# Marks of two edge sorts split over VectorE, ScalarE and GpSimd, and chunks placed one batch later on TensorE

## The reference

```python
logits = jax.nn.leaky_relu(al_s[src] + al_d[dst], 0.2)
alpha = _segment_softmax(logits, dst, num_nodes)
msg = h[src] * alpha[:, :, None]
out = jax.ops.segment_sum(msg, dst, num_segments=num_nodes)
```

## Time and profile before

| | us |
|---|---|
| median of 3 runs | 13213.7 (13208.91 to 13229.04) |
| profiled execution, its time | 13124.58 |
| its span | 13122.8 |
| busy in the span: DVE | 8087.8 |
| busy in the span: PE | 7310.8 |
| busy in the span: POOL | 5296.6 |
| busy in the span: ACT | 580.3 |
| counting loops | 174.5 and 175.1 |
| ranking loops | 1028.0 and 1028.1 |

### The profile page before, as it was taken

How to read it: one execution, slowest core, us unless ns; L and a number is a source line. 1 busy time by engine, 2 the same in 40 slices (tenths; PEclk the granted TensorE clock), 3 DMA queues, 4 the chain that set the end, 5 groups by cost and what they waited for, 6 DMA issues and landing times. The chain is left out here.

```text
span 13122.8 us, 152037 instructions
## 1 busy us (share of the span) xinstructions
PE 7310.8 (56%) x32826; PEld 4771.1 (36%) x32826; DVE 8087.8 (62%) x27204; ACT 580.3 (4%) x2200; POOL 5296.6 (40%) x5059
## 2 busy tenths in 40 slices
PE   4555355568886455556665466666666433333335
PEld 2333233344444344433333234444443323223333
DVE  9999899957777444445665666666664322332224
ACT  0000000010001000001000100000001000000001
POOL 0000000046662566615777033333330666556670
PEclk6777677765655555557666776666665555555557
DMA  0111111133332221213444133333330111211111
GB/s 18 50 50 51 38 50 50 53 93 107 106 106 53 60 43 42 42 10 105 114 111 110 64 113 112 112 112 111 111 102 31 45 45 45 38 20 23 23 23 22
DMA packets 456540, 857.24 MB, mean 65 GB/s; under 512 B 136865, under 2 KB 197974, under 8 KB 455766
## 3 DMA queue, kind: packets, MB, share of 16 engines
q0 software_dynamic: 226304, 550.69, 17.4%
q1 hardware_dynamic: 229718, 300.70, 7.8%
HBM read 798.81 MB, written 52.14 MB: 65 GB/s over the span
## 5 line engine op out<-in xcount | busy, mean ns | idle before, releaser
L954 POOL DMA_INDIRECT all_Y<-table,te_index x832 | 851.1, 1023 | 1384.9 <-DVE all_Y L1123 1177.1
L954 POOL DMA_INDIRECT all_Y<-table,a1e_index x832 | 891.3, 1071 | 454.6 <-issue 245.4
L954 POOL DMA_INDIRECT all_Y<-table,be_index x832 | 942.0, 1132 | 292.9 <-issue 245.8
L954 POOL DMA_INDIRECT all_Y<-table,a2e_index x832 | 833.0, 1001 | 515.5 <-DVE all_Y L1123 293.1
L1330 POOL DMA_INDIRECT g2e_rows<-table,g2e_index x832 | 839.6, 1009 | 447.1 <-issue 247.8
L1330 POOL DMA_INDIRECT g1e_rows<-table,g1e_index x832 | 815.4, 980 | 481.5 <-issue 236.0
L994 PE MATMUL te_ps_u<-all_Y,te_onehot 128*128 128x264 f32 x1664 | 749.1, 566 | 458.1 <-DVE all_Y L1123 384.2
L1123 DVE TENSOR_TENSOR all_Y<-all_Y 128x512 f32<-128x512 f32 (+1 forms) x1664 | 964.6, 580 | 40.3 <-issue 18.1
L994 PE MATMUL be_ps_u<-all_Y,be_onehot 128*128 128x258 f32 x1664 | 722.7, 572 | 430.0 <-DVE all_acc L1135 257.5
L994 PE MATMUL a1e_ps_u<-all_Y,a1e_onehot 128*128 128x264 f32 x1664 | 878.8, 654 | 83.8 <-DVE all_acc L1135 47.2
L1346 PE MATMUL g1e_ps_u<-g1e_rows,g1e_onehot 128*128 128x128 f32 x1664 | 485.1, 444 | 757.8 <-issue 478.3
(11 more groups left out here) (464 smaller groups left out, 15600.2 us busy)
## 6 DMA issues: line engine op xcount, KB each, us to landing
all_Y<-lows SPq DMA_DIRECT2D x196, 256.0 KB
all_Y<-codes SPq DMA_DIRECT2D x196, 256.0 KB
a1e_place_row<-places_dst SPq DMA_DIRECT2D x104, 256.0 KB
a2e_place_row<-places_dst SPq DMA_DIRECT2D x104, 256.0 KB
be_place_row<-places_src SPq DMA_DIRECT2D x104, 256.0 KB
te_place_row<-places_src SPq DMA_DIRECT2D x104, 256.0 KB
all_Y<-table,a1e_index POOLq DMA_INDIRECT x832
all_Y<-table,a2e_index POOLq DMA_INDIRECT x832
```

The costliest lines, as they stand in the source:

```text
L954: pool.indirect_dma_start(out=rows[:, r, k, :], out_offset=None, in_=table, in_offset=bass.IndirectOffsetOnAxis(ap=index[:, r, k:k + 1], a ...
```

## The change

In the counting loop DVE makes five of the eight low marks and ACT three: ACT takes the absolute difference of lane number and low part (`Abs`), three instructions of 128 columns, and then one `Relu` of 1 minus that, 384 columns. PE waits for both engines.

In the ranking loop ACT makes all low marks in that way, eight `Abs` and one `Relu` of 1024 columns, two batches ahead, and after them copies the eight values of that batch per partition from `other_t` into `carried`. POOL makes the row marks, eight `tensor_scalar` instructions a batch, from `row` (DVE) and `carried` (ACT). DVE keeps the column marks, now one behind the other, and has six of the next batch's `earlier` instructions in pairs where the low marks were, two at the end. In PE's step t the chunks of batch t-1 are placed, four ahead of the starts of t+1 and four behind; the last batch is placed after the loop. There are new semaphores for it, and two new buffers (`away`, `carried`).

```diff
--- before.py
+++ after.py
@@ -252,6 +252,7 @@
         m = Memory(nc, stack, f"count_{name}")
         in_acc = Region(acc)
         low1 = [in_acc.take(8, P, dt=F16) for _ in range(2)]
+        away = in_acc.take(8, P, dt=F16)
         window1 = [in_acc.take(8, WIN, dt=F16) for _ in range(2)]
         count = in_acc.take(WIN)
         groups = in_acc.take(WIN)
@@ -271,7 +272,8 @@
         ps_b = [m.ps(f"ps_b{h}", [P, 512]) for h in range(2)]
         s_marks, s_counted, s_count, s_sums, s_step, s_ends, s_turned, s_end, s_end1, s_windows = (m.sem(x) for x in (
             "marks", "counted", "count", "sums", "step", "ends", "turned", "end", "end1", "windows"))
-        s_hot, s_started, s_starts, s_prefix = (m.sem(x) for x in ("hot", "started", "starts", "prefix"))
+        s_hot, s_started, s_starts, s_prefix, s_away, s_late = (m.sem(x) for x in ("hot", "started", "starts", "prefix", "away", "late"))
+        SPLIT = 5
         with nc.Block() as block:
             @block.vector
             def _(dve):
@@ -279,7 +281,7 @@
                     wait(dve, s_counted, t - 1)
                     dve.tensor_tensor(window1[b], bc(lane16[:, 0:WIN].rearrange("p (k w) -> p k w", k=1), [P, 8, WIN]),
                                       bc(window_t[:, bass.ds(t * 8, 8)].rearrange("p (k w) -> p k w", w=1), [P, 8, WIN]), ALU.is_equal)
-                    for k in range(8):
+                    for k in range(SPLIT):
                         last = dve.tensor_scalar(low1[b][:, k, :], lane16[:, 0:P], low_t[:, bass.ds(t * 8 + k, 1)], None, ALU.is_equal)
                     last.then_inc(s_marks, 1)
 
@@ -332,10 +334,27 @@
                 link(dve.tensor_tensor_scan(starts, total, bc(c.zero[:, :], [P, NSLOT]), -1.0, ALU.add, ALU.add))
                 link(dve.tensor_tensor(place, place, starts, ALU.add))
 
+            @block.scalar
+            def _(act):
+                def marks(t, b):
+                    wait(act, s_late, t)
+                    for k in range(SPLIT, 8):
+                        act.activation(away[:, k, :], lane16[:, 0:P], ACT.Abs, scale=-1.0, bias=low_t[:, bass.ds(t * 8 + k, 1)]).then_inc(s_away, 1)
+                    wait(act, s_counted, t - 1)
+                    act.wait_ge(s_away, t * (8 - SPLIT) + (8 - SPLIT))
+                    act.activation(low1[b][:, SPLIT:8, :], away[:, SPLIT:8, :], ACT.Relu, scale=-1.0, bias=1.0).then_inc(s_late, 1)
+
+                marks(0, 0)
+                marks(1, 1)
+                with act.Fori(1, NB // 2) as i:
+                    marks(i * 2, 0)
+                    marks(i * 2 + 1, 1)
+
             @block.tensor
             def _(pe):
                 def tally(t, b, first=False, final=False):
                     pe.wait_ge(s_marks, t + 1)
+                    pe.wait_ge(s_late, t + 1)
                     for k in range(8):
                         last = pe.matmul(ps_c[:, 0:WIN], low1[b][:, k, :], window1[b][:, k, :], start=first and k == 0, stop=final and k == 7)
                     last.then_inc(s_counted, 1)
@@ -376,6 +395,7 @@
         code_row = [in_y.take(8 * P, dt=F16) for _ in range(2)]
         turned = [in_y.take(8 * P, dt=F16) for _ in range(2)]
         low1 = [in_y.take(8, P, dt=F16) for _ in range(2)]
+        away = in_y.take(8, P, dt=F16)
         window1 = [in_acc.take(8, WIN, dt=F16) for _ in range(2)]
         ahead = [in_acc.take(8, WIN, dt=F16) for _ in range(2)]
         picked = in_acc.take(8, WIN)
@@ -395,7 +415,8 @@
         s_turned, s_earlier, s_marks, s_prefix, s_ahead, s_total, s_high, s_base, s_start, s_picked, s_started, s_slot, s_scaled, s_column, s_row, s_hot, s_placed = (
             m.sem(x) for x in ("turned", "earlier", "marks", "prefix", "ahead", "total", "high", "base", "start", "picked", "started", "slot",
                                "scaled", "column", "row", "hot", "placed"))
-        s_step, s_passed = m.sem("step"), m.sem("passed")
+        carried = [in_acc.take(8) for _ in range(2)]
+        s_step, s_passed, s_away, s_low, s_value, s_valued, s_passed_pool = (m.sem(x) for x in ("step", "passed", "away", "low", "value", "valued", "passed_pool"))
 
         def batches(eng, step):
             step(0, 0)
@@ -432,8 +453,8 @@
                 def arrived(t, b):
                     dve.wait_ge(s_rows[b], t * 16 + (32 - 16 * b))
 
-                def earlier_in_chunk(t, b):
-                    for k in range(8):
+                def earlier_in_chunk(t, b, k0, k1):
+                    for k in range(k0, k1):
                         dve.scalar_tensor_tensor(same[:, k, :], code_row[b][:, k * P:(k + 1) * P], code_t[:, bass.ds(t * 8 + k, 1)], before,
                                                  ALU.is_equal, ALU.mult, accum_out=earlier[b][:, k:k + 1]).then_inc(s_earlier, 1)
 
@@ -458,45 +479,32 @@
                         dve.tensor_tensor(low16, base, high16, ALU.subtract).then_inc(s_base, 1)
                     if then:
                         dve.tensor_tensor(window1[n], bc(lane16[:, 0:WIN].rearrange("p (k w) -> p k w", k=1), [P, 8, WIN]),
-                                          bc(window_t[:, bass.ds(u * 8, 8)].rearrange("p (k w) -> p k w", w=1), [P, 8, WIN]), ALU.is_equal)
-
-                    def low_marks(k0, k1):
-                        for k in range(k0, k1):
-                            last = dve.tensor_scalar(low1[n][:, k, :], lane16[:, 0:P], low_t[:, bass.ds(u * 8 + k, 1)], None, ALU.is_equal)
-                        if k1 == 8:
-                            last.then_inc(s_marks, 1)
-
+                                          bc(window_t[:, bass.ds(u * 8, 8)].rearrange("p (k w) -> p k w", w=1), [P, 8, WIN]), ALU.is_equal).then_inc(s_marks, 1)
                     if now:
                         dve.wait_ge(s_started, t + 1)
                         dve.wait_ge(s_earlier, (t + 1) * 8)
                         dve.tensor_tensor(slot, start, earlier[b], ALU.add).then_inc(s_slot, 1)
                     if then:
-                        low_marks(0, 2)
+                        earlier_in_chunk(u, n, 0, 2)
                     if now:
                         dve.wait_ge(s_slot, t + 1)
                         dve.tensor_scalar(scaled, slot, 1.0 / P, -0.5 + 0.5 / P, ALU.mult, ALU.add).then_inc(s_scaled, 1)
                     if then:
-                        low_marks(2, 4)
+                        earlier_in_chunk(u, n, 2, 4)
                     if now:
                         dve.wait_ge(s_scaled, t + 1)
                         dve.tensor_scalar(column[b], scaled, MAGIC, -MAGIC, ALU.add, ALU.add).then_inc(s_column, 1)
                     if then:
-                        low_marks(4, 6)
+                        earlier_in_chunk(u, n, 4, 6)
                     if now:
                         dve.wait_ge(s_column, t + 1)
+                        wait(dve, s_valued, t * 8 - 8)
                         dve.scalar_tensor_tensor(row[b], column[b], -float(P), slot, ALU.mult, ALU.add).then_inc(s_row, 1)
-                    if then:
-                        low_marks(6, 8)
-                    if now:
                         for k in range(8):
                             wait(dve, s_placed, t * 8 + (k - 15))
-                            dve.tensor_scalar(column1[b][:, k, :], lane16, column[b][:, k:k + 1], None, ALU.is_equal)
-                            if k == 0:
-                                dve.wait_ge(s_row, t + 1)
-                            dve.tensor_scalar(row1[b][:, k, :], lane16[:, 0:P], row[b][:, k:k + 1], other_t[:, bass.ds(t * 8 + k, 1)],
-                                              ALU.is_equal, ALU.mult).then_inc(s_hot, 1)
+                            dve.tensor_scalar(column1[b][:, k, :], lane16, column[b][:, k:k + 1], None, ALU.is_equal).then_inc(s_hot, 1)
                     if then:
-                        earlier_in_chunk(u, n)
+                        earlier_in_chunk(u, n, 6, 8)
 
                 step(-1, 1)
                 batches(dve, step)
@@ -516,17 +524,44 @@
 
             @block.scalar
             def _(act):
+                def low_marks(u, b):
+                    wait(act, s_low, u)
+                    for k in range(8):
+                        act.activation(away[:, k, :], lane16[:, 0:P], ACT.Abs, scale=-1.0, bias=low_t[:, bass.ds(u * 8 + k, 1)]).then_inc(s_away, 1)
+                    act.wait_ge(s_away, u * 8 + 8)
+                    act.activation(low1[b], away, ACT.Relu, scale=-1.0, bias=1.0).then_inc(s_low, 1)
+                    wait(act, s_valued, u * 8 - 8)
+                    act.activation(carried[b], other_t[:, bass.ds(u * 8, 8)], ACT.Copy).then_inc(s_value, 1)
+
                 def step(t, b):
                     act.wait_ge(s_prefix, t + 1)
                     wait(act, s_start, t - 1)
                     act.activation(ahead[b].rearrange("p k w -> p (k w)")[:, WIN:8 * WIN], ps_r[b][:, WIN:8 * WIN], ACT.Copy).then_inc(s_ahead, 1)
-
+                    if exists(t + 2):
+                        low_marks(t + 2, b)
+
```

(28 more changed lines are left out.)

## The result

The changed kernel takes 13909.3 us (median of four runs, 13893.7 to 13911.8) against 13211.3 for the kernel before, also of four. The ratio is 1.0536, with a 95% interval of 1.0499 to 1.0573: 5.4% slower, where the forecast was 1.1% faster. (A ratio given here is the middle of its interval; the quotient of the medians can differ by 0.001 to 0.002, here it is 1.0528.) The profiled execution has a span of 13908.1 us.

A forecast was written before the change was run, and what follows sets the result against it. VectorE (DVE) was taken to bound both sorts' loops, with POOL the new ranking bound. Ranking -90, counting -69 and ends +12 gave -147 us from 13213.7, rounded 13,070 us; the 8-in-10 range was 12,780 to 13,390.

The forecast's parts named there:

- The ring: Ranking loop: DVE to `row`, POOL's eight marks, ACT's two copies, PE's starts, DVE wait in turn; 6.03 + 8p us a batch.
- 8p: Ranking loop: time of POOL's eight row marks in a batch, taken as 4.0 us.
- p: Ranking loop: distance between starts of two POOL row marks, taken as 0.50 us; at 0.56 the batch equals today's 10.49.
- high end: Ranking loop: a POOL mark that also waits for one DVE column mark each time, 0.47 + 0.35 = 0.82 us.
- POOL's begin: Ranking loop: delay from the end of DVE's `row` to POOL's first mark, 0.33 us.
- The starts: Ranking loop: PE's starts of the next batch, 0.74 us plus about 0.1 for first load and hand-over, 0.85 us.
- Rival 4: Ranking loop: PE's starts run at 1.2 GHz, 0.36 us more a batch, gain eaten; 13,140 to 13,240 us, chance 0.10.
- rival 2: Ranking loop: POOL's marks and DVE's column marks take turns at the port, 0.64 to 0.82 us each; 13,380 us, chance 0.33.
- Rival 3: Ranking loop: POOL is cheap, p = 0.29, ring 8.35 us; 12,740 us, or 12,560 at DVE's floor; chance 0.22.
- Counting: Counting loop: ACT's three `Abs` and one `Relu` set the batch at 1.43 us instead of 1.78, 69 us less in all.
- The ends: Ends of each sort: last batch placed after its last marks, first low marks ahead of first prefix; 12 us more in all.
- DVE's floor: Ranking loop: DVE keeps 7.4 us of work a batch; if it stayed the bound, 598 us would go.

The follow-up runs named there:

- e2: Changed kernel with the copy into `carried` made by DVE just ahead of `row` instead of by ACT; 12743.9 us, ratio 0.9659 to the kernel before.
- e4: Kernel before plus a block ahead of the sorts with POOL marks of several kinds; the mark takes 0.78 us alone, 1.1 beside DVE's column marks.
- e10: Changed kernel with twelve more 512-column matmuls a batch on PE ahead of the starts; 13762.5 us against 13135.9 for the kernel before, ratio 1.0485.
- e1: Changed kernel with row marks back on DVE and no `carried` copy; 12909.8 us against 13188.1 for the kernel before, ratio 0.9786.
- e7: e2 with six low marks of the counting loop on DVE and two on ACT; 12059.9 us, ratio 0.9609 to the kernel before.

## Why the prediction was wrong

**The mechanism was right.** The ring named in the prediction (DVE to `row`, POOL's marks, ACT's two copies, PE's starts) is the one that sets the batch; e2 cuts it, and 5.8 us a batch go. The time of a batch is a sum of the form that I wrote, a fixed part and 8p, but both parts were too small, so that the true break-even lies below the p = 0.56 that I gave.

**The failed step is the term 8p, the price of a POOL mark.** It stood at 4.0 us (p = 0.50, high end 0.82) and measured 7.31. Of the 3.3 us too little, 2.2 are POOL's own price (0.775 instead of 0.50) and 1.1 come from DVE's work beside it, nearly all from the column marks. I took the price per column of a `tensor_scalar` from a cast and added two reads for the pointers. e4 shows which half failed: the two pointers cost 0.14 us, near the 0.18 that I had put in, but "the comparison costs nothing extra" was wrong. With constants in place of pointers the mark still takes 4.9 / 8 = 0.61 us where the cast takes 0.29, and it grows by 3.3 ns a column instead of 0.8. Even my high end was too low, because it rested on the same row; and by the formula p = 0.82 makes 12.59 us a batch and 13,570 us, which the range, cut at 13,390, did not hold either. So the range failed although p was named as the open quantity: no row of the trace had this operation on POOL, and here the cast was only a lower bound.

**The other terms of the ring.** DVE's 4.19 us measured 4.17. ACT's copies, 0.66, measured 0.69. POOL's begin, 0.33, took 0.48; three waits stand ahead of the first mark, but no run takes them apart. The starts, 0.85, took 1.45, at the lower clock. Rival 4 had named this and priced it at 0.36 more, which is what came back from 1.45 to 1.09 in the turns of e10 whose clock rose. The other 0.24 is a reading that was too low at either clock. Together these add 0.15 + 0.60 + 0.03 - 0.02 = 0.76 us to the 3.3, and 10.03 becomes 14.10. They are small beside 8p, but they alone would have turned the sign. With 6.79 in place of 6.03 the break-even is p = 0.46, so that my p of 0.50 would have given 10.79 us a batch: 196 x 0.30 = 59 us more, less 21 for the counting, about 13,250 us. That lies in the range and is slower than the kernel before, not faster.

**The rivals.** The sign was that of rival 2, but not its cause or size. It would have had 13,380 us, with turns of 0.70 each. Of its signs one came, marks over 0.6 us apart, and the other did not: the column marks lasted 0.44 us as before. The port costs 0.14 us a mark here; if it had cost nothing, the ring would still have been 13.0 us a batch and the kernel slower. The Trainium skill (SBUF — State Buffer, "Who interferes with whom") has the second to issue blocked for the whole instruction of the other. The runs agree that the two interfere, and in both directions, but three column marks passed in one POOL mark of e4 (24 in 8.8 us, eight POOL marks beside them). So they do not take turns instruction by instruction, and with column marks POOL waits more than DVE. Rival 3 (cheap POOL) was the opposite of what came. Rival 4's sign came (the starts took over 1 us), as a part of the loss.

**Counting.** 21 us came instead of 69. A batch is 1.67 us, not 1.43: the `Abs` lasts 0.39 and the next starts 0.29 later. My row for it was a copy from PSUM with no pointer. The estimate from the Trainium skill (ScalarE: Activation LUTs, "What ACT_TABLE_LOAD costs"), 1.67 us, was the measured value. For the three `Abs` that is the page's price (0.39 us at 128 columns, each next one 0.29 later); that the whole fits to 0.01 us is partly luck, as the `Relu` took 0.52 us and the hand-over 0.17, which I had not measured. The row had been the wrong one.

**The ends.** They were priced at 12 us and cost about 2: PE's last placing starts at 3284.9 instead of 2597.0 us, 688 us later, of which 686 are the loops.

**DVE's floor.** 7.4 us of own work was right to 0.05 (e1: 9.19 with the row marks on it). With POOL working all the time it is 8.25, not 7.4, as e2 and e7 show: the gain of moving work from DVE to POOL is partly paid back on DVE.

## What to carry to other kernels

Before moving work to another engine, look at what stands behind each wait in the queue of every engine that will wait for it. A copy of 0.2 us waited on ACT for GpSimd's marks with the next batch's `ahead` behind it, and cost 5.8 us a batch; issued by an engine that needs to wait there anyway, it cost 0.1. And price an operation by a row of the same operation on the same engine. If there is none, as with `tensor_scalar` on GpSimd here, take the row of another operation for no more than a lower bound and leave much room above it: here the cast took 0.29 us and the mark 0.78 alone, 0.91 beside DVE. And sum the small terms of a ring with the same care when the forecast sits near its break-even: here 0.76 us of them were enough to turn the sign.

## What the runs showed of the hardware

- GpSimd's `tensor_scalar` with a comparison and a multiplication takes 0.775 us for 128 columns, f16 and f32 alike, 3.77 us for 1024 (e4). VectorE makes the same mark in 0.22. GpSimd's copy of the same tile takes 0.25 us (e4).
- VectorE's f16 column marks of 832 columns beside it slow GpSimd from 0.775 to 1.1 us and are themselves 0.37 instead of 0.35 us apart (e4). VectorE's two-input L458 is slowed from 0.27 to 0.41 us while GpSimd works (e2), but not every one: the second of each pair kept 0.27, and so did the pair behind the column marks, beside which GpSimd's mark took 0.90 instead of 0.775.
- ScalarE's `Abs` with a pointer bias, 128 columns of SBUF, lasts 0.39 us and lets the next begin after 0.29 (counting loop of the changed kernel); a copy of the same width from PSUM without a pointer let it begin after about 0.17 (two of 0.28 took 0.45 together).
- PE's 23 starts, with no matmul for 7 us before them, run at a granted clock of 0.50 and span 1.12 us; with twelve wide matmuls a batch put in before them, e10 runs them at 1.00 within 0.6 us in most turns and at 0.50 in the slow one shown.
